# Two pipeline slots earlier: the first expert tiles of a ViT tower beside the last three LSTM steps

## The chip, the cores and the metric

The kernel is one program on one core of one Trainium2 chip. The core has TensorE (PE, matmuls), VectorE (DVE), ScalarE (ACT), GpSimd (POOL) and SyncE (SP, which here only issues DMAs). The metric is the device time of one execution in microseconds (us), the median of three runs of the kernel before.

## The reference, cut to what matters

Three layers on 128 images. Each image becomes T = 65 tokens of width 128 (a class token and 64 patches of 2352 values times W); the tokens are normalized and go through an LSTM over the 65 positions, whose output is added; the sum is normalized again and goes through 16 experts, of which each token uses its best two.

```python
tokens = einsum('bpi,hi->bph', patches, W) + b          # 64 patches an image
h = concat([cls, tokens]) * pos_embed
def step(carry, xt):                                    # 65 steps, one after the other
    gates = xt + h @ W_hh.T
    i, f, g, o = sigmoid, sigmoid, tanh, sigmoid
    c = f * c + i * g;  h = o * tanh(c)
h = h + lstm(layernorm(h))
probs = softmax(xt @ router_w.T + router_b); top 2 of 16
def expert_step(acc, e):                                # 16 experts
    h = gelu(xt @ w1e.T + b1e, approximate=False)       # 128 -> 512
    y = h @ w2e.T + b2e                                 # 512 -> 128
    acc + y * gate
```

## The kernel before, in words

Everything is written as slots n = -5, -4, ..., which each engine goes through in the same order. In a slot an engine runs its part of `step(n)` and, from some slot on, its part of `step_b` for a tile. The function `slots(step, tile)` says how they are put together: up to slot AHEAD = 64 the step comes first and the tile behind it, from slot 65 on the tile first. POOL has its step first in every slot.

`step(n)` is LSTM step n (n = 0 to 64) with all that belongs to it: the projection of the patches of token n+3 (PE L1287, until slot 61), the recurrent matmuls (PE L1297 and L1302), the four gates as tanh (ACT L610), `cab` and `c2` (DVE L809, L812), tanh of the cell (ACT L631), the new hidden state in two float16 parts and one float32 (DVE L831, L833, L837), the transposition of step n-1's hidden state (PE L1312), its sum with the token `h1` (DVE L787), the moments for the norms (DVE L791 to L805), their power -0.5 (POOL L1253), `shift2` (DVE L817), the normalized payload `pay` (ACT L644), the router's logits (PE L1388), and, spread over slots, the router's choice of experts and the ranks of the rows in them (DVE, groups of 8, 6, 4, 4 and 3 tokens). Each token's row is sent twice into the area `sent` of its experts by indirect DMAs on POOL (L1241). What of this belongs to the last tokens stands in slots 65 to 74. A plan, made in pieces on DVE, says for each tile of 256 rows which expert it has and where its rows begin: the early plan (tiles 0 to 23) is read in slot 55, pieces 8 and 9 of it follow in slots 61 and 62, and the late plan (tiles 24 to 79) takes slots 72 to 78, from PLAN_B = 72 on.

`step_b(n)` is tile n of 80. SP loads its rows three slots ahead (`xt`, L537, for which tile j waits for `dst_done` of tile j-4) and the bias b2 one slot ahead (L547, for which tile j waits for `y_done` of tile j-4). One slot ahead PE transposes the rows (L1416) and DVE splits them into two halves (L1113, L1127). In the tile's own slot PE makes the 512-wide layer (L1442, two halves of 6 matmuls of 256 columns), ACT applies gelu (L685, four of 128x256) and rounds to float16 (L694, one of 128x1024), and DVE makes the destination numbers (L1138). One slot later DVE makes the rest (L1105), two slots later PE makes the second layer (L1460, 24 matmuls), three slots later DVE adds the bias (L1120) and POOL scatters the rows into `back` by two indirect DMAs (L1265). Tile 0 is in slot 64: tile n is in slot n + 64.

The first x loads and the matmuls of a tile use memory that the patches had, and PSUM banks that the steps have. So tile 0 waits for the last projection and tiles 0 and 1 for the last gates. SP also writes padding rows behind every expert's rows (L505), two of them in each of eight slots from PLAN_B + 4 on; tile 24's load waits for all of these and for all sent rows.

`warm` (L633) is a gelu of one element at the end of step 64. The instruction that loads ACT's function table for gelu is put before it by the compiler.

Near the end tiles' results are read back in chunks (L511), weighted and added (L674, L1189), and stored (L517).

Of the kernel before, what the change touches and what calls it, by code (L numbers as in the profile page):

```python
# [24 lines left out]
P = 128  # L25
# [28 lines left out]
THIN = 4  # L54
THREE = 3
EARLY = 24
SINGLE_IN, SINGLE_DOWN = 16, 5
AHEAD = 64
assert EARLY <= -(-(2 * P * sum(SIZES[:EARLY_GROUPS]) - E * (ROWS - 1)) // ROWS)
NX = 4  # L60
NPOS = 4
# [36 lines left out]
def tower(nc, x, w, w_rest, cls, pos, w_ih, w_hh, b_ih, b_hh, rw, rb, we, b1, b2, const, out):  # L98
# [3 lines left out]
    with ctx:  # L102
# [147 lines left out]
            return max([i for i in range(j) if alternates(i, single) == alternates(j, single)], default=None)  # L250

        def ps_in(j):
            return bank[6 if alternates(j, SINGLE_IN) else 0][:, 0:ROWS]

        def ps_down(j):
            return bank[4 if alternates(j, SINGLE_DOWN) else 1][:, 0:HALVES * HID]

        def ps_up(n, half):

            return bank[(3, 7, 2, 5)[2 * (n % 2) + half]]  # L260

        def ps_ranks(g, a, b):

# [55 lines left out]
        STARTS = np.cumsum([0] + SIZES).tolist()  # L319
        def slots(step, tile, steps_first=False):  # L320

            for n in range(-5, AHEAD + TILES_B + 4):
                if n <= AHEAD or steps_first:
                    step(n)
                if n >= AHEAD - 3:
                    tile(n - AHEAD)
                if n > AHEAD and not steps_first:
                    step(n)

# [67 lines left out]
        PLAN_AT = {47: 0, 48: 1, 49: 2, 50: 3, 51: 4, 52: 5, 54: 6, 55: 7, 61: 8, 62: 9}  # L397
        LATE_AT = {PLAN_B + k: at for k, at in enumerate(((0,), (1,), (2,), (3,), (4, 5), (6,), (7,)))}
        DIAGONALS_AT = {54: False, PLAN_B + 5: True}
        assert ready(EARLY_GROUPS - 1) < 47 and 52 < ready(EARLY_GROUPS) and 55 <= AHEAD - 3  # L400
        assert PLAN_B + 4 + E // 2 <= AHEAD + EARLY - 3

        def pieces_of(n):

# [41 lines left out]
        def _(sp):  # L446
# [20 lines left out]
            def step(n):  # L467
                t = n + 6
                if 2 <= t <= T - 1:
                    if t <= NX:  # L470
                        sp.wait_ge(ones_in, t)
                    else:
                        sp.wait_ge(tok_done, (t - NX))
                        sp.wait_ge(lo_done, (t - NX))
                    load_patches(t)
                t = n + 4
                if 0 <= t <= T - 1:
                    if t >= NPOS:
                        through(sp, h0_done, t - NPOS)
                    sp.dma_start(posr[:, t % NPOS, :],  # L480
                                 pos[bass.ds(t, 1), :].rearrange("a h -> (a h)").partition_broadcast(P)
                                 ).then_inc(pos_in[t % NPOS], 16)
                if n == -4:
                    for dst, src in ((wih[:, :, :], w_ih), (whh[:, :, :], w_hh),
                                     (lbias[:, 0, :], b_ih), (lbias[:, 1, :], b_hh)):
                        sp.dma_start(dst, src).then_inc(weights_in, 16)
                if n == -3:
                    for dst, src in ((rws[:, :], rw), (rbs[:, :, :], rb.partition_broadcast(P)), (b1s[:, :], b1)):
                        sp.dma_start(dst, src).then_inc(const_in, 16)
                for piece in pieces_of(n + 2):  # L490
                    if piece >= NE:
                        through(sp, ex_lo_done, piece - NE)
                    sp.dma_start(ex_raw[:, piece % NE, :], we[:, bass.ds(piece * PIECE, PIECE)]
                                 ).then_inc(ex_in[piece % NE], 16)
                if n == 10:
                    sp.wait_ge(setup_dve, 2)
                    sp.dma_start(rows_of(sent, E * CAP), pad[:, :, :]).then_inc(pads, 16)
                for e in range(2 * (n - PLAN_B - 4), 2 * (n - PLAN_B - 3)):
                    if not 0 <= e <= E - 1:
                        continue  # L500
                    if e == 0:
                        sp.wait_ge(pad_rows, 1)
                    sp.reg_load(at_pad, padi[0:1, e:e + 1])
                    row = sp.snap(at_pad, min_val=0, max_val=E * CAP - ROWS)
                    sp.dma_start(rows_of(sent, row), pad[:, :, :]).then_inc(pads, 16)  # L505
# [66 lines left out]
        def _(act):  # L572
# [30 lines left out]
            def step(n):  # L603
# [25 lines left out]
                if 0 <= n <= T - 1:  # L629
                    through(act, c_done, n)  # L630
                    act.activation(tc[:, :], c2, ACT.Tanh, scale=0.5).then_inc(tc_done, 1)  # L631
                    if n == T - 1:
                        act.activation(warm[:, :], cst[:, C_ONE:C_ONE + 1], ACT.Gelu)  # L633
                if halved:
                    split(t, KS // 2, KS).then_inc(hi_done, 1)
                if n == -2:
# [22 lines left out]
                for k, (t0, t1, at) in enumerate(SOFTMAX):  # L659
                    if n == at + 1:  # L660
                        exponents(k, t0, t1)

            def exponents(k, t0, t1):

# [24 lines left out]
            def round_off(n):  # L689

                act.wait_ge(gelu_done, 2 * n + 2)
                if n >= 4:
                    through(act, down_ps, n - 4)
                act.activation(hhi[n % 4], pair[n % 2][:, :], ACT.Copy).then_inc(hhi_done, 1)  # L694

            def step_b(n):
                if 0 <= n <= TILES_B - 1:
# [21 lines left out]
        def _(dve):  # L719
# [382 lines left out]
            def remainder(n):  # L1102

                through(dve, hhi_done, n)
                dve.tensor_tensor(hlo[n % 4], pair[n % 2][:, :], hhi[n % 4], ALU.subtract).then_inc(hlo_done, 1)  # L1105

            def step_b(n):
                j = n + 1
# [163 lines left out]
        def _(pe):  # L1272
# [17 lines left out]
            def step(n):  # L1290
# [15 lines left out]
                if 0 <= t <= T - 1:  # L1306
                    through(pe, h_done, t)
                    if t >= 1:
                        through(pe, h1_done, t - 1)
                    if t == T - 1:  # L1310
                        through(pe, yT_done, t - 2)
                    pe.transpose(ps_hT(t), h2[:, t % 2, :], ident).then_inc(h_ps, 1)  # L1312
# [91 lines left out]
            def step_b(n):  # L1404
                j = n + 1
                if 0 <= j <= TILES_B - 1:

                    pe.wait_ge(xt_in[j % 4], (j // 4 + 1) * 16)
                    if j == 0:
                        through(pe, h0_done, T - 1)  # L1410
                    if previous(j, SINGLE_IN) is not None:
                        through(pe, in_done, previous(j, SINGLE_IN))
                    elif j > 0:
                        pe.wait_ge(plan_read, 2)
                    for a in range(HALVES):
                        last = pe.transpose(ps_in(j)[:, a * P:(a + 1) * P], xt[j % 4][:, a, 0:HID], ident)  # L1416
                    last.then_inc(in_ps, 1)
                if 0 <= n <= TILES_B - 1:
# [6 lines left out]
                    through(pe, in_done, n)  # L1425
                    x_hi, x_lo = xTs[n % 2][:, 0:ROWS], xTs[n % 2][:, ROWS:2 * ROWS]
                    for half in range(2):
                        if n >= 2:
                            through(pe, hlo_done, n - 2)
                        elif half == 0:  # L1430
                            through(pe, gates_done, T - 2 + n)
                        elif n == 0:
                            g = max(k for k in range(GROUPS) if ready(k) <= AHEAD)
                            pe.wait_ge(r_dve, g * R + R_MASK + 2)
                            pe.wait_ge(plan_read, 1)
                        else:
                            through(pe, h1_done, T - 2)
# [71 lines left out]
```

## Time and profile before

| | |
|---|---|
| median of 3 runs | 673.73 us (673.32 to 677.51) |
| the profiled execution | 673.6 us, span 671.8 us |
| PE busy | 621.2 us (92%) |
| DVE busy | 562.6 us (84%) |
| ACT busy | 489.5 us (73%) |
| POOL busy | 412.7 us (61%) |

The span is what the profile covers, 1.8 us less than the time of the same execution. Three stretches follow each other: the LSTM steps until 399 us, with the projections beside them until 385.4; the tiles until 651.5; and the last reading back, adding and storing. A busy share is a mean over all three.

### The profile page before, as it was taken

What the parts mean: (1) busy time and instruction counts of PE and PEld (TensorE: products, weight loads), DVE (VectorE), ACT (ScalarE), POOL (GpSimd) and SP (SyncE); (2) the same over time, 40 slices, a digit from 0 to 9 for tenths busy, and PEclk for the clock granted to TensorE, in tenths of its full rate; (3) what the DMA queues carried; (4) which work ended last, traced back from release to release, by engine and by line L of the source; (5) the groups of instructions that cost most, each with busy time, mean ns of one, the idle gap of its engine ahead of it and who ended that gap; (6) DMA issues with size and microseconds to landing.
All of it is one profiled execution on the core that took longest, in us unless ns stands there. A gap on an engine that the chain in (4) does not pass through costs nothing.

```text
span 671.8 us, 24556 instructions
## 1 busy us (share of the span) xinstructions
PE 621.2 (92%) x7952; PEld 588.0 (88%) x7952; DVE 562.6 (84%) x1797; ACT 489.5 (73%) x1259; POOL 412.7 (61%) x446
## 2 busy tenths in 40 slices
PE   5899999999999999999999978999999999999970
PEld 4899999999999999999999957788888989888860
DVE  3877888888888888988989978987777887989896
ACT  3687778666667776665655567777888888999984
POOL 0233333477777776667657777777776666666571
PEclk9999999999999999999999979999999999999995
DMA  8988787677888888877767123456444345555666
GB/s 312 384 293 270 271 276 258 230 259 270 268 276 274 269 270 260 251 232 253 253 217 252 56 64 95 116 155 183 135 119 117 118 109 159 161 171 163 189 223 203
DMA packets 71895, 141.67 MB, mean 211 GB/s; under 512 B 13078, under 2 KB 55650, under 8 KB 63838
## 3 DMA queue, kind: packets, MB, share of 16 engines
q1 hardware_dynamic: 62128, 121.69, 57.0%
q0 software_dynamic: 9280, 17.21, 7.3%
q8 instruction: 70, 1.15, 0.7%
q10 hardware_dynamic: 366, 1.21, 0.5%
q14 instruction: 51, 0.42, 0.2%
HBM read 116.35 MB, written 25.66 MB: 211 GB/s over the span
## 4 chain that ended last, share of the span: by engine, by line
PE 59%; DVE 7%; issue 5%; DMA 5%; SPq 2%; POOL 2%; ACT 1%; POOLq 0%; ACTq 0%; DVEq 0%
PE pair L1287 24%; PE pair L1442 10%; PE pair L1460 10%; PE pair L1333 4%; DMA patches<-sent 4%; PE pair L1297 3%; PE pair L1416 2%; DVE patches L1105 2%; PE pair L1302 1%; POOL back L1265 1%; PE pair L1388 1%; DMA field<-back 1%; PE pair L1322 1%; PE pair L1359 1%; PE pair L1312 1%
## 5 line engine op out<-in xcount | busy, mean ns | idle before, releaser
L1265 POOL DMA_INDIRECT back<-patches x160 | 156.7, 979 | 70.7 <-issue 58.2
L1287 PE MATMUL pair<-field,patches 128*128 128x128 f32 (+1 forms) x1408 | 173.6, 280 | 8.4 <-DMA patches<-in_x 8.4
L1241 POOL DMA_INDIRECT sent<-pay,slot_own x130 | 149.7, 1152 | 40.2 <-issue 38.0
L1287 PEld LDWEIGHTS pair<-field,patches 128*128 128x128 f32 (+1 forms) x1408 | 164.4, 194 | 8.6 <-ACT field L584 6.8
L685 ACT ACTIVATE pair<-pair,b1s 128x256 f32<-128x256 f32 x320 | 123.2, 448 | 31.1 <-PE pair L1442 30.3
L610 ACT ACTIVATE gate<-pair,lbias 128x128 f32<-128x128 f32 x260 | 74.1, 367 | 81.0 <-PE pair L1302 79.1
L1442 PE MATMUL pair<-patches,ex_hi 128*128 128x256 f16 x640 | 111.2, 276 | 6.1 <-DVE patches L1105 3.6
L1460 PE MATMUL pair<-ex_hi,patches 128*128 x1280 | 111.4, 219 | 2.9 <-DVE patches L1105 1.5
L1253 POOL TENSOR_TENSOR rstd<-veps,cst 128x2 f32<-128x2 f32 (+1 forms) x68 | 57.4, 845 | 90.7 <-DVE veps L805 89.5
L1105 DVE TENSOR_TENSOR patches<-pair,patches 128x1024 f16<-128x1024 f32 x80 | 97.0, 1212 | 1.3 <-ACT patches L694 1.3
L1287 PE MATMUL pair<-field 128*128 128x128 f16 x1536 | 96.1, 219 | 0.0
L1460 PEld LDWEIGHTS pair<-ex_hi,patches 128*128 128x128 f16 x1280 | 87.0, 98 | 6.4 <-issue 3.7
L1287 PEld LDWEIGHTS pair<-field 128*128 128x128 f16 x1536 | 91.3, 98 | 0.9
L1460 PE MATMUL pair<-ex_lo,patches 128*128 x640 | 88.0, 219 | 0.0
L1442 PE MATMUL pair<-patches,ex_lo 128*128 128x256 f16 x320 | 87.9, 275 | 0.0
L592 ACT ACTIVATE field<-patches 128x512 f16<-128x512 f32 x128 | 80.7, 632 | 4.5 <-DMA patches<-in_x 4.5
L694 ACT ACTIVATE patches<-pair 128x1024 f16<-128x1024 f32 x80 | 81.9, 1023 | 2.5
L848 DVE TENSOR_TENSOR field<-patches,field 128x1024 f16<-128x1024 f32 x64 | 78.0, 1219 | 0.1
L1442 PEld LDWEIGHTS pair<-patches,ex_hi 128*128 x640 | 55.9, 98 | 24.9 <-issue 14.5
L1215 POOL TENSOR_TENSOR ex_lo<-field,ex_hi 128x256 f16<-128x256 f32 x64 | 45.4, 720 | 43.4 <-ACT field L658 43.0
L1113 DVE CAST patches<-pair 128x256 f16<-128x256 f32 x80 | 33.8, 422 | 35.0 <-PE pair L1416 34.0
L1333 PE MATMUL pair<-xT_hi,wih_hi 128*128 128x128 f16 x260 | 47.4, 220 | 2.9 <-DVE xT_lo L765 2.9
(150 smaller groups left out, 1232.2 us busy)
## 6 DMA issues: line engine op xcount, KB each, us to landing
patches<-in_x SPq DMA_DIRECT2D x62, 1152.0 KB
patches<-sent SPq DMA_DIRECT2D x80, 130.0 KB
field<-in_we SPq DMA_DIRECT2D x64, 128.0 KB
field<-back SPq DMA_DIRECT2D x10, 768.0 KB
patches<-in_b SPq DMA_DIRECT2D x80, 64.0 KB
field<-in_pos SPq DMA_DIRECT2D x65, 64.0 KB
out_tower<-h SPq DMA_DIRECT2D x10, 384.0 KB
back<-patches POOLq DMA_INDIRECT x160
```

The costliest lines, as they stand in the source:

```text
L592: return act.activation(xhi[r][:, a:b, :], xraw[q][:, a:b, :], ACT.Copy)
L610: last = act.activation(gate[:, GATE_AT[g], :], ps_gate[n % 2][:, g * B:(g + 1) * B], ACT.Tanh, bias=lbias[:, 2, g:g + 1], scale=(1.0 if g ...
L685: last = act.activation(up[:, cols], up[:, cols], ACT.Gelu, bias=b1s[:, bass.ds(e * FC + 2 * half + i, 1)], scale=1.0 / E_SCALE)
L694: act.activation(hhi[n % 4], pair[n % 2][:, :], ACT.Copy).then_inc(hhi_done, 1)
L848: dve.tensor_tensor(xlo[r][:, :, :], xraw[q][:, 0:KS, :], xhi[r][:, :, :], ALU.subtract).then_inc(lo_done, 1)
L1105: dve.tensor_tensor(hlo[n % 4], pair[n % 2][:, :], hhi[n % 4], ALU.subtract).then_inc(hlo_done, 1)
L1241: pool.indirect_dma_start(sent, bass.IndirectOffsetOnAxis(ap=slot_own[:, g % 4, choice, col:col + 1], axis=0), pay[:, t % NP, :], None, bo ...
L1265: pool.indirect_dma_start(back, bass.IndirectOffsetOnAxis(ap=dsti[j % NO][:, k:k + 1], axis=0), yo[j % NO][:, k, :], None, bounds_check=2 ...
L1287: last = pe.matmul(bank_of, l, w_, start=(c == KS and k == 0), stop=(c == KS - 1 and k == 2))
L1333: pe.matmul(ps_gate[t % 2][:, g * B:(g + 1) * B], w_[:, g, :], r[:, t % 2, :], start=(g == 0 and k == 0), stop=False, skip_group_check=True)
L1442: last = pe.matmul(ps_up(n, half)[:, i * ROWS:(i + 1) * ROWS], w1, r, start=(k == 0), stop=(k == 2))
L1460: last = pe.matmul(ps_down(j)[:, a * HID:(a + 1) * HID], h, w2, start=(c == 0 and k == 0 and a == 0), stop=(c == FC - 1 and k == 2), skip_ ...
```

## The change

Tile n is in slot n + 62 (`FIRST = AHEAD - 2`), so that tiles 0, 1 and 2 are in slots 62, 63 and 64, behind the LSTM steps of these slots. The steps keep their slots, the padding rows keep their tiles (from slot PLAN_B + 2 on, and so two slots earlier). Because steps 62 to 64 still use their PSUM banks, the first three tiles get others: their rows are transposed into the upper half of the bank of the hidden states, and their 512-wide layer has pair 2, pair 0, pair 1 of banks in turn. The single-element gelu stands at the end of slot 61. Waits follow the banks: the transposition of hidden states 61 to 63 waits for the split of tile 0 to 2, tile 0's layer waits for the last token's `h0`, tile 1's and 2's first half for the gates of steps 63 and 64. From tile 18 instead of 16 on two banks take turns for the transposed rows.

```diff
-SINGLE_IN, SINGLE_DOWN = 16, 5
+SINGLE_IN, SINGLE_DOWN = 18, 5
 AHEAD = 64
+FIRST = AHEAD - 2
+UPPER = 3
...
         def ps_in(j):
+            if j < UPPER:
+                return ps_h[:, 2 * P:2 * P + ROWS]
             return bank[6 if alternates(j, SINGLE_IN) else 0][:, 0:ROWS]
...
+        def ps_pair(n):
+            return pair[(n + 1) % 2 if n else 2]
         def ps_up(n, half):
-            return bank[(3, 7, 2, 5)[2 * (n % 2) + half]]
+            return ps_pair(n)[:, half * 512:(half + 1) * 512]
...
-            for n in range(-5, AHEAD + TILES_B + 4):
+            for n in range(-5, FIRST + TILES_B + 4):
                 if n <= AHEAD or steps_first:
                     step(n)
-                if n >= AHEAD - 3:
-                    tile(n - AHEAD)
+                if n >= FIRST - 3:
+                    tile(n - FIRST)
...
-                for e in range(2 * (n - PLAN_B - 4), 2 * (n - PLAN_B - 3)):
+                for e in range(2 * (n - PLAN_B - 2), 2 * (n - PLAN_B - 1)):
...
-                    if n == T - 1:
-                        act.activation(warm[:, :], cst[:, C_ONE:C_ONE + 1], ACT.Gelu)
...
+                if n == FIRST - 1:
+                    act.activation(warm[:, :], cst[:, C_ONE:C_ONE + 1], ACT.Gelu)
...
-                act.activation(hhi[n % 4], pair[n % 2][:, :], ACT.Copy).then_inc(hhi_done, 1)
+                act.activation(hhi[n % 4], ps_pair(n)[:, :], ACT.Copy).then_inc(hhi_done, 1)
...
-                dve.tensor_tensor(hlo[n % 4], pair[n % 2][:, :], hhi[n % 4], ALU.subtract).then_inc(hlo_done, 1)
+                dve.tensor_tensor(hlo[n % 4], ps_pair(n)[:, :], hhi[n % 4], ALU.subtract).then_inc(hlo_done, 1)
...
                         through(pe, h1_done, t - 1)
+                    if FIRST - 1 <= t < FIRST - 1 + UPPER:
+                        through(pe, in_done, t - FIRST + 1)
...
-                    if j == 0:
-                        through(pe, h0_done, T - 1)
-                    if previous(j, SINGLE_IN) is not None:
+                    if j < UPPER:
+                        through(pe, h1_done, FIRST - 2 + j)
+                    if j == UPPER:
+                        through(pe, hlo_done, 0)
+                    elif previous(j, SINGLE_IN) is not None:
...
-                        if n >= 2:
+                        if n >= UPPER:
                             through(pe, hlo_done, n - 2)
+                        elif n == 0:
+                            through(pe, h0_done, T - 1)
                         elif half == 0:
-                            through(pe, gates_done, T - 2 + n)
-                        elif n == 0:
+                            through(pe, gates_done, T - 3 + n)
+                        elif n == 1:
```

## Rows read from the trace of the kernel before

**Rows 1.** The page's busy times by engine: busy us, share of span, instructions

```profile
PE 621.2 (92%) x7952; PEld 588.0 (88%) x7952; DVE 562.6 (84%) x1797; ACT 489.5 (73%) x1259; POOL 412.7 (61%) x446
```

**Rows 2.** Stretches: length, busy us of PE, PEld, DVE, ACT, POOL, clock, DMA, GB/s

```profile
388.00:390.00 2.00, 0.39 (x5) 0.39 (x6) 1.86 (x9) 0.82 (x3) 1.63 (x2) 1.00 0.31 88
392.00:394.00 2.00, 2.00 (x18) 1.69 (x16) 1.45 (x7) 0.61 (x3) 1.64 (x5) 0.52 0.11 35
...
508.00:540.00 32.00, 32.00 (x416) 28.81 (x413) 26.84 (x59) 27.86 (x55) 20.82 (x23) 1.00 0.40 114
```

**Rows 3.** ACT in order of time: start us, us, line and operation

```profile
386.32 1.14 ACT L610 ACTIVATE gate<-pair,lbias 128x128 f32<-128x128 f32 x4 [1.43 <-PE pair L1302]
...
391.00 1.14 ACT L610 ACTIVATE gate<-pair,lbias 128x128 f32<-128x128 f32 x4 [0.74 <-PE pair L1302]
...
392.96 0.31 ACT L631 ACTIVATE tc<-gate 128x128 f32<-128x128 f32 x1 [0.65 <-DVE gate L812]
394.29 0.49 ACT L644 ACTIVATE pay<-h,shift,rstd 128x128 f32<-128x128 f32 x1 [1.03 <-DVE shift L817]
394.69 1.13 ACT L610 ACTIVATE gate<-pair,lbias 128x128 f32<-128x128 f32 x4
...
397.13 1.28 ACT L633 ACT_TABLE_LOAD   x1
398.43 0.20 ACT L633 ACTIVATE warm<-cst 128x1 f32<-128x1 f32 x1
...
400.88 1.02 ACT L694 ACTIVATE patches<-pair 128x1024 f16<-128x1024 f32 x1
401.80 1.53 ACT L685 ACTIVATE pair<-pair,b1s 128x256 f32<-128x256 f32 x4
...
404.37 1.54 ACT L685 ACTIVATE pair<-pair,b1s 128x256 f32<-128x256 f32 x4
```

**Rows 4.** ACT's groups from 386 to 399 us: busy us, mean ns, idle before

```profile
L610 ACT ACTIVATE gate<-pair,lbias 128x128 f32<-128x128 f32 x12 | 3.4, 367 | 2.2 <-PE pair L1302 2.2
L644 ACT ACTIVATE pay<-h,shift,rstd 128x128 f32<-128x128 f32 x3 | 1.5, 488 | 1.8 <-DVE shift L817 1.8
L631 ACT ACTIVATE tc<-gate 128x128 f32<-128x128 f32 x3 | 0.9, 309 | 2.1 <-DVE gate L812 2.1
```

**Rows 5.** DVE in order of time, from 385 to 441 us

```profile
387.37 0.17 DVE L805 TENSOR_SCALAR veps<-mv 128x2 f32<-128x2 f32 x1
387.50 0.42 DVE L809 SCALAR_TENSOR_TENSOR cab<-gate 128x256 f32<-128x256 f32 x1
...
400.36 0.42 DVE L1113 CAST patches<-pair 128x256 f16<-128x256 f32 x1 [1.17 <-PE pair L1416]
400.82 0.42 DVE L1127 TENSOR_TENSOR patches<-pair,patches 128x256 f16<-128x256 f32 x1
401.93 1.22 DVE L1105 TENSOR_TENSOR patches<-pair,patches 128x1024 f16<-128x1024 f32 x1 [0.69 <-ACT patches L694]
...
433.58 0.41 DVE L1120 SCALAR_TENSOR_TENSOR patches<-pair,patches 128x256 f32<-128x256 f32 x1
...
439.89 0.41 DVE L1120 SCALAR_TENSOR_TENSOR patches<-pair,patches 128x256 f32<-128x256 f32 x1
```

**Rows 6.** The chain of waits in order of time: start us, us, what

```profile
397.23 2.68 PE pair L1442 x12
...
416.21 1.35 PE pair L1442 x12
417.56 1.34 PE pair L1460 x24
```

**Rows 7.** SP in order of time: the first padding rows, the load of tile 24

```profile
441.73 1.19 SPq L505 DMA_DIRECT2D sent<-pad  x2
...
472.37 0.33 SPq L537 DMA_DIRECT2D patches<-sent  x1
```

**Rows 8.** POOL in order of time: the last row sent before tile 24

```profile
447.45 0.97 POOL L1241 DMA_INDIRECT sent<-pay,slot_own  x1 [0.30 <-issue]
```

More of the change, by code:

```diff
@@ L399, in tower @@
         DIAGONALS_AT = {54: False, PLAN_B + 5: True}
-        assert ready(EARLY_GROUPS - 1) < 47 and 52 < ready(EARLY_GROUPS) and 55 <= AHEAD - 3
-        assert PLAN_B + 4 + E // 2 <= AHEAD + EARLY - 3
+        assert ready(EARLY_GROUPS - 1) < 47 and 52 < ready(EARLY_GROUPS) and 55 <= FIRST - 3
+        assert PLAN_B + 2 + E // 2 <= FIRST + EARLY - 3
         def pieces_of(n):
```

## The prediction

> **What bounds the kernel now.** I read the busy times first, and they mislead: PE is busy 92% of the span [rows 1], but the change touches some 20 us around the end of the LSTM, so the question is what ends each wait there. The stretches come next. In 388 to 390 us PE works for 0.39 of 2.00 us, and in 392 to 394 its clock is granted at 0.52, which is the lower of its two levels (1.2 of 2.4 GHz), after that idling [rows 2]. So there is a hole in PE beside steps 62 to 64. Later there is none: from 508 to 540 PE is busy for all 32 us with 416 matmuls; a tile has 38 (2 + 12 + 24), which makes 10.95 tiles and 2.92 us a tile. That is the price of a slot once PE sets the pace.
>
> Then ACT in order of time. The gates of step 63 start at 391.00, those of step 64 at 394.69: a step lasts 3.69 us, and it is a chain of short pieces, gates 1.14, wait 0.65 for `c2`, tanh 0.31, wait 1.03 for `shift2`, pay 0.49, gates again [rows 3]. Step 62 lasts 4.68 (386.32 to 391.00). No engine is full in this chain. ACT's groups show it: from 386.3 it idles for 2.1 + 1.8 us and, of L610's 2.2, for the 0.74 that lie behind 386.32, some 4.7 us in all [rows 3, 4]. From 400.88 on ACT works tile after tile: gelu 401.80, gelu 404.37, a period of 2.57 us [rows 3]. From 401.93 on DVE takes over, as it has the router's work of slots 65 to 78 beside the tiles: its rest of tile 0 starts at 401.93 [rows 5], just behind ACT's rounding (400.88 + 1.02). In slots 76 to 83 SP has the padding rows, two issues of 1.19 us together in each slot beside two loads, the first at 441.73, and tile 24's load goes out at 472.37 [rows 7]. After that PE sets the pace until the tail.
>
> **The change part by part.** The tail and everything from tile 24 on are bound to tile numbers, not slots. So the result is one sum: how much later slot 65 comes (slots 62 to 64 now carry three tiles), against two tile slots less, 2 x 2.92 = 5.84 us.
>
> *The function table.* Load and warm are 1.28 + 0.20 us [rows 3]. They leave the end of step 64, where pay would wait for its shift anyway, and go to the end of slot 61, where ACT idles 1.43 us before 386.32. Cost there 0.05 to 0.2 us, I take 0.1.
>
> *Slot 61, tile 0's rows.* PE's two transposes (some 0.3 us) come before step 62's matmuls, so gates 62 start 0.25 later. DVE's split of the rows takes 400.36 to 401.24, 0.88 us [rows 5], and now stands before DVE's work of step 62. DVE was at its limit there: `veps` 387.37 to 387.54 and `cab` at 387.50 follow each other without a gap [rows 5]. So `c2` and all behind it in step 62 are 0.85 late, and ACT is through with the step at about 391.1.
>
> *Slot 62, tile 0.* PE has its transposes for tile 1 and the reading of the expert's number (0.3 to 0.5 us) and starts the 12 matmuls at about 391.2. They take 2.68 us at the low clock, as tile 0's did at 397.23, and 1.35 at the high one [rows 6]. The first gelu pair needs half of them. With the high clock gelu runs from 391.9, rounding ends at 394.5 (period 2.57), and gates 63 start at 394.6. With the low clock the second half is ready only at 393.9, and gates 63 start at 395.9. Before it was 391.00.
>
> *Slots 63 and 64.* ACT is in program order: gates, tanh, pay, gelu, gelu, rounding, gates. Gelu stands behind pay, and the next gates behind the rounding, so that tile work doesn't go into ACT's waits within a step, it is added: 3.69 + 2.57 = 6.26 us a step. Tile 1's matmuls wait for gates 63 (1.14), then take 1.35 to 2.68: ready at 2.5 to 3.8 after the start of the gates, needed in two halves at 3.69 and 4.5, and so hidden. In the same way tile 2's. Slot 64's rounding ends at 394.6 + 12.5 = 407.1, or 408.4. Before, slot 64's ended at 401.90. DVE has in slot 64 the state (0.9 us after tanh), shift, split 0.88, rest of tile 1 1.22, in slot 65 the split with the bias of tile 0 and reaches the rest of tile 2 at 407.4, which puts the first case up by 0.3. Slot 65 is later by **5.5 to 6.5 us**.
>
> *Slots 65 and 66.* Two things are new there. The bias sum (0.41, of which 0.33 counts as the next overlaps) was not yet there in slot 66's place, and in slot 65 PE has the second layer of tile 1, 1.34 us [rows 6], before the transposition of hidden state 64, for which DVE waits some 0.4. Together 0.7: **6.2 to 7.2 us**. All else that DVE does in slots 65 to 74 is the same as before.
>
> *Padding rows and SP.* SP gets to them in slot 74 instead of 76, released by the bias sum of tile 9. In the old slots 74 and 76 that sum lies at 433.58 and 439.89 [rows 5], 6.31 apart, more than 5.84, since DVE's slots were long. So SP starts 6.2 to 7.2 less 6.31 later, that is 0.1 earlier to 0.9 later, and from there on it has its own work (30.6 us from 441.73 to 472.37 for the same 8 slots [rows 7]) beside which DVE's late plan is hidden; some 0.2 us, in which SP still waited for DVE, can go. That gives **-0.3 to +0.7 us** for tile 24 and for everything behind it. The middle is +0.2.
>
> *POOL.* Its two scatters of a tile come two slots earlier in its queue, so four of them (1.27 us each: 0.97 and 0.30 idle) stand before the last sent rows, 5.1 us. With the 5 us that POOL now waits for the longer steps, the last send goes from 447.45 [rows 8] to 453 to 458. Tile 24 needs it at 472.37: covered by 14 us; if that cover were gone, each further send would cost 1.27. The power that feeds the shift is better off, since steps are longer. The other banks and the change from 16 to 18 cost nothing: the banks that tiles 0 to 2 leave are free when they are needed, and the split of a row tile is done a slot before.
>
> The sum: 673.6 + 0.2 = **673.8 us** for an execution like the profiled one, which is 0.1 below the median of 673.73; I take 673.8.
>
> **The rivals.** *ACT's holes are filled.* If the gates, tanh and gelu of a slot fell so that waits shrink, the bound is ACT's work: 3 tiles x 2.57 = 7.7 us against 4.7 us of idling [rows 4] and the 1.48 of the table that leave this place, 1.5 us more in place of 5.5. Then slot 65 is only 2.2 late, SP starts 6.31 - 2.2 = 4.1 earlier and the time is 669.5. The order gelu behind pay speaks against all of it; half of it would be 671.6. Chance 0.15.
>
> *PE stays slow.* The idling of PE ahead of 390 us brings the low clock [rows 2]. If it stays low through slots 62 to 66, matmuls of a tile end at 4.1 us after its gates start, and those of the next step (0.5 us at the high clock) behind them by another 0.5; three steps and slot 65 make 1.5 to 2 us above my sum: 675.5. It decides once a tile's second half is ready later than 4.5 us after the gates. Chance 0.12.
>
> *The tables.* This is the rival on the slower side. The trace has three table loads; tanh, exp, Copy and Identity ran under the first, gelu, Copy and Identity under the second. No row has a tanh under gelu's table. If it doesn't hold tanh, steps 62 to 64 need a load before their first tanh and one before their gelu: 6 x 1.28 = 7.7 us [rows 3], every one in ACT's chain: 681.2. It decides with the first tanh of step 62. For tanh in the table speaks only that a table held four functions here; chance 0.07. The Trainium skill (ScalarE: Activation LUTs, "Table sets: the hidden batching unit") lists tanh beside exp and beside sigmoid, and for the gelu set no further function, which speaks against this change. By its figure of about 2.66 us a switch (What ACT_TABLE_LOAD costs) the time would be 689.5; the trace has the next instruction 0.02 us behind a load of 1.28.
>
> *The tiles don't move.* If tile 0's chain waits for something that comes with step 64 anyway, slots 62 to 64 stay as they were and the tiles follow as now: 673.6, the same as my forecast to within what can be measured. For tile 4's load this is nearly so: SP waits for tile 0's destination numbers, but needs them later. Chance 0.06.
>
> **How the numbers follow.** My sum has 0.60; its own range is 672.8 to 674.8, the two ends with 0.5 us on both sides for what rows round off. For 8 in 10 the range has to take in half of the first rival and the slow clock: **670.5 to 676.2**; it leaves out the tables and the full filling. A difference below 1% (6.7 us) cannot be told from no change here. Faster by over 1% would need 666.9, below the price of ACT's full filling: 0.02. Slower by over 1% is the table rival: 0.07. Within 1%: 0.91.
>
> **What the new profile would show.** Gates 63 start at 394.6 to 395.9 instead of 391.00, steps 63 and 64 last 6.3 us; the rounding of tile 2 ends at 407 to 408.5; one table load before 386.5 and no other until the last exp; tile 24's load at 472 +- 0.6; PE busy without a gap from there, the same tail. My prediction is wrong if a step with a tile lasts much less than 6.3 us (then ACT's waits were filled), or if SP's padding slots are not the same length as now, which would shift everything behind them.

## The result, and the profile after

The changed kernel takes 677.89 us (median of 20 runs, 673.9 to 679.39) where the kernel before, on the same chips, takes 675.16 (20 runs, 673.32 to 677.51). The ratio is 1.0032, 95% interval 1.0018 to 1.0045: some 2.2 us slower, clear of zero and far inside 1%. The median of the three runs shown ahead of the prediction lay low (673.73). The profiled execution has a span of 675.4 us, 3.6 more than before.

All times below are read against the tanh of the cell in step 61, the last piece on ScalarE ahead of the moved work. It starts at 382.28 us before and at 382.93 here. This 0.65 is no effect of the change: over the executions profiled below the same piece starts 0.03 to 1.67 late, also where nothing ahead of slot 76 differs. I take it off and call what is left "later" or "earlier".

ACT in order of time in the changed kernel, against [rows 3]:

```profile
382.93 0.31 ACT L639 ACTIVATE tc<-gate 128x128 f32<-128x128 f32 x1 [1.14 <-DVE gate L820]
...
385.56 1.28 ACT L669 ACT_TABLE_LOAD   x1
...
393.17 0.81 ACT L693 ACTIVATE pair<-pair,b1s 128x256 f32<-128x256 f32 x2 [1.42 <-PE pair L1456]
394.24 0.81 ACT L693 ACTIVATE pair<-pair,b1s 128x256 f32<-128x256 f32 x2 [0.26 <-PE pair L1456]
395.08 1.02 ACT L702 ACTIVATE patches<-pair 128x1024 f16<-128x1024 f32 x1
396.00 1.14 ACT L618 ACTIVATE gate<-pair,lbias 128x128 f32<-128x128 f32 x4
...
402.29 1.14 ACT L618 ACTIVATE gate<-pair,lbias 128x128 f32<-128x128 f32 x4
403.29 0.30 ACT L627 ACTIVATE ynT<-pair 128x128 f32<-128x128 f32 x1
...
407.25 0.81 ACT L693 ACTIVATE pair<-pair,b1s 128x256 f32<-128x256 f32 x2 [0.25 <-PE pair L1456]
408.09 1.02 ACT L702 ACTIVATE patches<-pair 128x1024 f16<-128x1024 f32 x1
```

Gates 63 come at 396.00, that is 4.35 later than the 391.00 of before; gates 64 at 402.29, 6.95 later; step 63 lasts 6.29 us instead of 3.69. Gates 63 follow the rounding of tile 0 without a wait. One table load, and no other in steps 62 to 64.

The chain of waits from gates 64 on, against [rows 6]:

```profile
402.29 1.14 ACT gate L618 x4
403.42 0.18 ACT ynT L627
403.60 0.04 issue
403.64 0.61 PE pair L1398 x2
404.25 0.51 PE pair L1428 x2
404.76 2.35 PE pair L1456 x12
407.11 1.34 PE pair L1474 x24
408.45 0.23 PE pair L1428 x2
```

Here is what the sum of the prediction left out. After gates 64 the chain leaves ScalarE for TensorE: the logits wait for `ynT`, which stands behind the gates, and then TensorE has one queue of the rows of tile 3, tile 2's first layer at the low clock (2.35 us), tile 0's second layer and the rows of tile 4. The stretches show the clock, against [rows 2]:

```profile
400.00:402.00 2.00, 0.62 (x8) 0.39 (x5) 1.94 (x6) 1.97 (x5) 1.44 (x2) 1.00 0.10 33
402.00:404.00 2.00, 0.36 (x2) 0.36 (x3) 0.85 (x4) 1.59 (x6) 1.34 (x2) 0.83 0.44 107
404.00:406.00 2.00, 2.00 (x11) 1.39 (x11) 1.49 (x7) 0.70 (x2) 1.39 (x3) 0.50 0.20 66
406.00:408.00 2.00, 2.00 (x26) 1.74 (x24) 1.63 (x3) 1.67 (x5) 1.70 (x2) 0.81 0.21 69
```

PE works 0.98 of the 4 us from 400 to 404 (from 400.6 to 403.6 it does nothing), and its clock is granted at 0.50 in the next two, the lower level. VectorE gets the rows of tile 4 late, against [rows 5]:

```profile
408.71 0.42 DVE L1121 CAST patches<-pair 128x256 f16<-128x256 f32 x1 [1.09 <-PE pair L1428]
...
409.72 1.21 DVE L1113 TENSOR_TENSOR patches<-pair,patches 128x1024 f16<-128x1024 f32 x1
```

The rest of tile 2 (slot 65) starts at 409.72, 7.14 later than slot 65's rest of before (401.93). Before, it followed ScalarE's rounding at once; here the rounding ends at 409.11, and VectorE comes 0.6 after it, because it waited for the rows of tile 4 from TensorE. The slot after it is 7.8 later, and every slot up to 78 then 7.8 to 8.1 later. Two slots at the pace of the padding stage are not enough to give this back, as SP shows, against [rows 7]:

```profile
444.04 1.20 SPq L513 DMA_DIRECT2D sent<-pad  x2
...
450.95 2.16 SPq L513 DMA_DIRECT2D sent<-pad  x2
...
475.34 0.33 SPq L545 DMA_DIRECT2D patches<-sent  x1
```

The first padding rows are 1.66 later than before, tile 24's load 2.32 later. From there the two kernels run in step: VectorE's rest of tile 24 is 2.44 later, that of tile 60 2.29, that of tile 79 2.89.

### The profile page after: what moved, and what is told of

The parts are those of the page before. It is cut to its first block, busy times and chain, and to the rows that moved or that the text cites. A ratio compares the mean times of both kernels' runs of the same rounds, so it can differ in the third digit from the quotient of the medians.

```text
span 675.4 us, 24556 instructions
## 1 busy us (share of the span) xinstructions
PE 622.1 (92%) x7952; PEld 589.6 (87%) x7952; DVE 562.5 (83%) x1797; ACT 490.2 (73%) x1259; POOL 412.7 (61%) x446
## 4 chain that ended last, share of the span: by engine, by line
PE 59%; DVE 7%; DMA 6%; issue 6%; POOL 2%; ACT 1%; SPq 1%; POOLq 0%; ACTq 0%; DVEq 0%
PE pair L1295 24%; PE pair L1456 10%; PE pair L1474 10%; DMA patches<-sent 4%; PE pair L1343 4%; PE pair L1305 3%; PE pair L1428 2%; DVE patches L1113 2%; PE pair L1310 1%; POOL back L1273 1%; PE pair L1398 1%; DMA field<-back 1%; PE pair L1332 1%; PE pair L1369 1%; PE pair L1322 1%
## 5 line engine op out<-in xcount | busy, mean ns | idle before, releaser
L1474 PEld LDWEIGHTS pair<-ex_lo,patches 128*128 128x128 f16 x640 | 49.2, 98 | 0.0
```

Source lines behind the costliest of these rows:

```text
L1474: last = pe.matmul(ps_down(j)[:, a * HID:(a + 1) * HID], h, w2, start=(c == 0 and k == 0 and a == 0), stop=(c == FC - 1 and k == 2), skip_ ...
```

## The experiments

The twelve runs are compared in a few places: VectorE's rest of tile 2, of tile 14 (in the padding stage), of tile 24 (behind it) and of tile 79, each in us later (+) or earlier (-) than the same tile in the kernel before. The stage from the first padding rows to tile 24's load, in us, says what SP's slots cost. The ratio is over 11 or 12 timed runs each (20 for the changed kernel), against the kernel before on the same chip.

| kernel | tile 2 | tile 14 | tile 24 | tile 79 | stage | ratio (95%) |
|---|---|---|---|---|---|---|
| before | 0 | 0 | 0 | 0 | 30.6 | 1 |
| changed | -1.22 | +1.13 | +2.44 | +2.89 | 31.3 | 1.0032 (1.0018 to 1.0045) |
| 1 table only | -0.25 | -0.16 | +0.16 | +0.37 | 30.8 | 0.9996 (0.9977 to 1.0014) |
| 2 one slot | +0.95 | +1.92 | +4.11 | +4.91 | 32.4 | 1.0041 (1.002 to 1.0063) |
| 3 ScalarE lags | -2.06 | +0.45 | +2.33 | +4.85 | 31.3 | 1.0023 (1.0001 to 1.0045) |
| 4 second layer early | -1.37 | +1.95 | +4.26 | +5.33 | 32.1 | 1.004 (1.002 to 1.0059) |
| 5 before, padding split | -0.19 | -0.08 | -1.57 | -0.38 | 28.9 | 0.9968 (0.995 to 0.9986) |
| 6 changed, padding split | +0.41 | +2.52 | +0.91 | +1.81 | 29.0 | 1.0005 (0.9986 to 1.0024) |
| 7 recurrence first | -2.84 | -0.27 | +0.36 | +0.67 | 30.5 | 1.0004 (0.9986 to 1.0023) |
| 8 = 7, padding split | -3.52 | -0.95 | -2.39 | -1.78 | 28.3 | 0.9981 (0.9963 to 1.0) |
| 9 changed, again | +0.25 | +2.63 | +3.58 | +7.99 | 30.8 | 1.0053 (1.0035 to 1.0072) |
| 10 clock kept up | -2.54 | +0.08 | +3.19 | +4.50 | 31.7 | 1.0038 (1.002 to 1.0055) |
| 11 = 8, clock kept up | -3.64 | -1.11 | -2.83 | -0.20 | 27.7 | 0.9978 (0.9962 to 0.9995) |
| 12 = 11, padding earlier | -3.69 | -1.13 | -2.89 | -1.53 | 30.4 | 0.9973 (0.9958 to 0.9988) |

In the kernel before, VectorE's rest of tile 2 comes 8.36 us behind that of tile 0, so 0 in the column "tile 2" would be a slot 65 that is 8.36 us later, and -1.22 is the 7.14 above. The stage of number 12 is one slot longer than the others, as its padding rows start a slot earlier for the same tile 24.

Each row is one execution, and one program differs from execution to execution. The changed kernel was profiled twice (+2.44 and +3.58 at tile 24), and up to tile 11 number 6 is a third execution of it: tile 2 lies at -1.22, +0.25 and +0.41. Behind tile 63, while results are read back, it is worse: number 9 loses 4.5 us between tiles 63 and 74 and number 3 2.8. So the readings go by tiles 2 to 24, differences of about 1 us between two rows settle nothing by themselves, and the ratio says what is left of them.

**1. The table load alone.** The kernel before, and only the load moved:

```diff
-                    if n == T - 1:
-                        act.activation(warm[:, :], cst[:, C_ONE:C_ONE + 1], ACT.Gelu)
...
+                if n == AHEAD - 3:
+                    act.activation(warm[:, :], cst[:, C_ONE:C_ONE + 1], ACT.Gelu)
```

> The kernel before with one part of the change: the single-element gelu, and so the load of its table, stands at the end of slot 61, and the tiles stay in slots 64 and on. If gelu's table holds tanh (my theory), there is one load before 386.5 us and none in steps 62 to 64, gates 62 start at most 0.2 us late, the rounding of tile 0 ends 0 to 0.4 us earlier than 401.9, and the time is that of before within 0.5 us. If it doesn't, three pairs of loads of 1.28 us stand in steps 62 to 64 and the time is 4 to 8 us longer.

The load is at 385.62 us, the twelve gates and three tanh behind it run with no other load, and the tiles are 0.25 earlier up to tile 13. The table that is loaded for gelu serves tanh too. The rival of the tables is out, and this part costs nothing that can be measured (0.9996).

**2. One slot instead of two.** `FIRST = AHEAD - 1`, tiles 0 and 1 with the banks of before, tile 0's rows in the bank of the hidden states, padding rows from PLAN_B + 3 on:

```diff
-FIRST = AHEAD - 2
-UPPER = 3
+FIRST = AHEAD - 1
+UPPER = 1
...
-            return pair[(n + 1) % 2 if n else 2]
+            return pair[n % 2]
```

> The change with one slot instead of two: tile n in slot n + 63, tiles 0 and 1 beside steps 63 and 64. Theory 'added, not hidden': a step with a tile lasts 6.3 us instead of 3.7, so slot 65 comes 3.3 to 4.0 us later than before for one tile slot of 2.92 won, and tile 24 is loaded 0.3 to 1.2 us later than before, half of the 2.3 us of the full change. Rival 'padding rows': what is lost is lost in SP's slots, whose number is the same; then the loss of tile 24 is near the full 2.3 us. Rival 'one hole is free': the first tile fits into waits, and tile 24 comes earlier than before.

Slot 65's rest is 3.51 later, inside the 3.3 to 4.0, but the one behind it is 4.77 later, and for tile 24 no side's number came: it is 4.11 later, more than in the full change. The first padding rows are 2.00 later; 1.8 us more arose in the padding stage (32.4 us instead of 30.6). The profile shows no clock fall in step 63 here, but one after step 64: TensorE does nothing from 397.0 to 400.3, and the clock is granted at 0.50 from 400 to 406 us. One tile beside the steps was enough for such a wait, and the time is no better than that of the full change (1.0041 against 1.0032, the intervals overlap).

**3. ScalarE lags.** In the changed kernel ScalarE's part of tiles 0 and 1 goes into the waits of steps 63 and 64, the first half of gelu ahead of the cell's tanh, the second behind it, the rounding behind `pay`; VectorE's rest of tile 0 now stands in step 64, ahead of its wait for the gates:

```diff
+                lagging = n - FIRST - 1 if FIRST < n <= T - 1 else None
+                if lagging is not None:
+                    e = expert_at(lagging)
+                    gelu(lagging, 0, e)
                 if 0 <= n <= T - 1:
...
                     act.activation(tc[:, :], c2, ACT.Tanh, scale=0.5).then_inc(tc_done, 1)
+                if lagging is not None:
+                    gelu(lagging, 1, e)
...
+                if lagging is not None:
+                    round_off(lagging)
```

> The change, with ScalarE's part of tiles 0 and 1 put one slot later and into its waits: in steps 63 and 64 the first gelu pair stands before tanh of the cell, the second behind it, the rounding behind pay; tile 2 follows in slot 65 before tile 3, and VectorE's rest of tile 0 stands before the first product of step 64. If ScalarE's program order is what makes a step with a tile 6.3 us long, gates 63 start at about 392.5, steps 63 and 64 last 4.6 to 5.2 us, and the rest of tile 2 on VectorE starts at 404.5 to 406 instead of 409.7; tile 24 is loaded 3 to 4.5 us earlier than in the change, and the time is 0.5 to 2.5 us below before. If the slots behind 64 or SP's padding rows are the bound, the gain is gone by tile 24 and the time is that of the change, 2 to 3 us above before.

Half of what was expected came. Step 63 lasts 4.61 us (396.15 to 400.76), as expected. But gates 63 don't come sooner:

```profile
396.15 1.15 ACT L618 ACTIVATE gate<-pair,lbias 128x128 f32<-128x128 f32 x4 [4.28 <-PE pair L1325]
...
400.76 1.13 ACT L618 ACTIVATE gate<-pair,lbias 128x128 f32<-128x128 f32 x4
```

ScalarE waits 4.28 us for the recurrent matmuls of step 63 (L1325 here), which stand behind tile 0's first layer on TensorE (12 matmuls in 2.5 us, at the low clock). So gates 63 come at the same time by either of two orders, ScalarE's and TensorE's. Taking away one leaves the other. My expectation had only one.

**4. Second layer of tile 0 in step 64's hole**, in TensorE's step ahead of the logits:

```diff
+                if n == FIRST + 2:
+                    second_layer(0)
```

> The change, with one piece moved: the second layer of tile 0 (24 matmuls) stands in step 64 on TensorE, ahead of the logits, in the 3.0 us in which TensorE waited, instead of behind tile 2's first layer. If the low clock and this order cost what I read from the profile, TensorE keeps its high clock, tile 2's 12 matmuls take 1.35 instead of 2.35 us, and the rest of tile 2 starts 0.9 to 1.5 us earlier (408.2 to 408.8 by the profile of the change); tile 24 and the end gain as much. If ScalarE alone sets the pace there, the gain is at most 0.3 us.

Counted as above, tile 2's rest is only 0.15 earlier than in the changed kernel, which looks like a miss. But this execution came late to the edit: up to step 64 the program is the changed kernel, and tile 0's first layer happened to take 2.7 us instead of 1.9, so that gates 63 and 64 start 0.84 and 0.89 later than in the first profile. From gates 64 on it did what was expected:

```profile
402.80 1.13 ACT gate L618 x4
...
409.20 1.23 DVE L1113 TENSOR_TENSOR patches<-pair,patches 128x1024 f16<-128x1024 f32 x1
```

The clock stays at the high level from 396 to 414 us, tile 2's first layer takes 1.48 us, and the rest of tile 2 comes 6.4 us after gates 64 and at once behind ScalarE's rounding. In the three executions with the order of the change it comes 7.4, 8.0 and 9.0 us after gates 64. Further on the gain is lost (+4.26 at tile 24): TensorE slows at 414.8 us (24 matmuls of the second layer in 2.04 us), and the padding stage takes 32.1 us. The time is not better (1.004).

**5 and 6. Every second padding DMA on ScalarE's queue** (the lines with `e` odd stand in ScalarE's step), in the kernel before and, with `PLAN_B - 2` for `PLAN_B - 4`, in the changed one:

```diff
-                for e in range(2 * (n - PLAN_B - 4), 2 * (n - PLAN_B - 3)):
+                for e in range(2 * (n - PLAN_B - 4), 2 * (n - PLAN_B - 3), 2):
...
+                e = 2 * (n - PLAN_B - 4) + 1
+                if 0 <= e <= E - 1:
...
+                    act.reg_load(at_pad, padi[0:1, e:e + 1])
+                    row = act.snap(at_pad, min_val=0, max_val=E * CAP - ROWS)
+                    act.dma_start(rows_of(sent, row), pad[:, :, :]).then_inc(pads, 16)
```

> The kernel before; every second padding-row DMA is issued by ScalarE's queue instead of SyncE's, in the same slots. If SyncE's issuing (3.5 to 4.2 us a slot, eight slots) is what sets the pace from tile 12 to tile 24, a slot there falls to VectorE's or TensorE's 2.95 to 3.5 us, tile 24 is loaded 2 to 4 us earlier than 472.4, and the time falls by as much. If what is slow is the DMA engines' own work on the padding rows (16 DMAs of 130 KB), it is the same within 0.7 us.

> The changed kernel with the same edit. Theory 'two losses': 1.5 us come from slots 62 to 65 and are there before the padding rows, 0.8 us come in SyncE's slots. With SyncE relieved, tile 24 is 2.5 to 4.5 us earlier than in the change, and against the kernel before with the same edit the loss is what VectorE's slots give, 0.5 to 1.9 us. Rival 'it is all SyncE': the two kernels with this edit are equal within 0.5 us at tile 24.

Tile 24 comes 1.57 earlier in the kernel before and 1.53 earlier in the changed one (+0.91 instead of +2.44). SP's issuing does set the pace there, for less than I expected (2 to 4 and 2.5 to 4.5). And the change costs as much with the padding split as without: 2.48 and 2.44 us at tile 24, by the ratios 0.37% and 0.32% (so close an agreement at tile 24 is luck, as one program differs by more). So the rival "it is all SyncE" falls, and so does my theory's 0.5 to 1.9; what is lost with the padding split is made ahead of the padding rows (first rows 2.98 later, stage 29.0 against 28.9) and passed on. Number 5 is faster than the kernel before, clear of zero. Number 6 also shows chance: it is the changed kernel until slot 74, yet its tile 2 is 1.6 later than in the first profile, and its low clock lasted longer. The chain has tile 2's first layer in 2.56 us and tile 0's second layer in 2.56 as well:

```profile
404.22 2.56 PE pair L1464 x12
406.78 2.56 PE pair L1482 x24
```

**7 and 8. The recurrence first**, on both engines, without and with the split padding. Tile n - 63's first layer stands on TensorE behind step n's recurrent matmuls, the first half of its gelu on ScalarE behind the cell's tanh, and the rest behind `pay`; VectorE's rest of tile 0 as in number 3:

```diff
+                if n in (FIRST + 1, FIRST + 2):
+                    first_layer(n - FIRST - 1)
...
                     act.activation(tc[:, :], c2, ACT.Tanh, scale=0.5).then_inc(tc_done, 1)
+                if lagging is not None:
+                    e = expert_at(lagging)
+                    gelu(lagging, 0, e)
...
+                if lagging is not None:
+                    gelu(lagging, 1, e)
+                    round_off(lagging)
```

> The change with both orders turned round in steps 63 and 64: TensorE does the recurrent matmuls of the step first and the first layer of the tile before (tile 0 in step 63, tile 1 in step 64) behind them; ScalarE does its gelu behind tanh of the cell, one slot later than in the change, tile 2 following in slot 65. If gates 63 started late (396.0) only because TensorE did tile 0's 12 matmuls at the low clock first, they start at 391.8 to 392.8 now, and gates 64 at 397.5 to 399 instead of 402.3. The rest of tile 2 starts 1.5 to 4 us earlier than in the change, and tile 24 1 to 3.5 us earlier. If what is taken out there only comes back behind slot 64, tile 24 is the same within 0.7 us.

> The kernel of the third run with the padding rows split between SyncE and ScalarE as in the first two. If the two losses are independent, it gains over the change what the two edits gain alone, 4 to 7 us at tile 24, and is 1.5 to 4 us faster than the kernel before. If one hides the other, it is no better than the better of the two.

ACT in number 7:

```profile
392.35 1.14 ACT L618 ACTIVATE gate<-pair,lbias 128x128 f32<-128x128 f32 x4 [0.79 <-PE pair L1324]
...
396.57 0.81 ACT L700 ACTIVATE pair<-pair,b1s 128x256 f32<-128x256 f32 x2 [0.77 <-PE pair L1479]
...
399.44 1.14 ACT L618 ACTIVATE gate<-pair,lbias 128x128 f32<-128x128 f32 x4
```

Gates 63 start 0.9 later than before instead of 4.35, gates 64 4.3 later instead of 6.95. Tile 2's rest is 1.6 earlier than in the changed kernel, tile 24's 2.1: the loss of the change is gone (+0.36, ratio 1.0004), and so it came from the order in the queues in steps 62 to 64. Step 63 did not get shorter by this (7.09 us, as tile 0's matmuls still met the low clock, 0.50 from 394 to 396); what was won is that it starts 3.5 us sooner. TensorE's order was not turned round alone: number 3 has ScalarE's and VectorE's, number 7 all three. With the padding split too, tile 24 is 2.39 earlier than before, 4.83 earlier than in the changed kernel, more than the two edits gained alone (2.1 and 1.5). The time, 0.9981, is 1.3 us better than before, a little less than the 1.5 to 4 I expected, and its interval reaches to no difference.

**9 and 10. The changed kernel again, and with the clock kept up** by matmuls of no use:

```diff
+                if n == 64:
+                    through(pe, r_logits, 8)
+                for _ in range({62: 34, 64: 38}.get(n, 0)):
+                    pe.matmul(ps_logit[:, 256:384], wih_hi[:, 0, :], wih_hi[:, 1, :], start=True, stop=True,
+                              skip_group_check=True)
```

> The changed kernel as it is, once more, beside the next two. It says how far one execution differs from another: I expect gates 63 at 4.2 to 4.5 us later than before, counted from step 61's tanh, slot 65's rest 6.9 to 8.5 us later, as TensorE's low clock in slots 64 and 65 ends at another moment in each execution, and tile 24 2 to 4 us later.

> The changed kernel with matmuls that do nothing of use (float16, 128 columns, into columns nobody reads) on TensorE in its two waits: 34 in step 62 behind the ranks, 38 in step 64 ahead of the logits. If the low clock costs what I read, the clock stays at the high level, tile 0's and tile 2's 12 matmuls take 1.35 to 1.5 us instead of 1.9 and 2.35, gates 63 start 0.4 to 1.2 us earlier, and slot 65's rest on VectorE 1.3 to 2.5 us earlier than in the change; tile 24 gains as much and the loss against before falls from 2.4 to 0 to 1.1 us. If the clock is only a companion of waits that ScalarE's order sets, slot 65 is the same within 0.4 us.

Number 9 was expected at 4.2 to 4.5 for gates 63 and has 5.11; its slot 65, at 8.61, lies just above 8.5. The stretches of number 10 have the clock at 1.00 from 388 to 412 us. Gates 63 start at 395.16, which is 4.03 later than before (4.35 in the first profile, 5.11 in number 9), step 63 lasts 6.28 as ever, and tile 2's rest is 1.32 earlier than in the first profile and 2.79 earlier than in number 9. Against number 6 it is 2.95. So the low clock costs 1.3 to 2.95 us in slots 62 to 65 of the changed kernel, and differs by 1.6 from one execution to the next. As in number 4, the rest of tile 2 follows ScalarE's rounding at once in number 10; in the first profile, number 9 and number 6 it comes 0.6, 1.4 and 2.0 after it. In number 9 the low clock sits later:

```profile
404.00:406.00 2.00, 1.42 (x10) 1.08 (x11) 1.37 (x5) 0.56 (x3) 1.70 (x2) 0.94 0.38 119
406.00:408.00 2.00, 2.00 (x15) 1.59 (x13) 1.97 (x5) 1.63 (x4) 1.39 (x3) 0.50 0.16 50
408.00:410.00 2.00, 2.00 (x25) 1.96 (x24) 0.28 (x3) 1.50 (x3) 1.61 (x2) 0.71 0.26 58
```

The gain is still there at tile 14 (+0.08) and then it goes: tile 24 is 3.19 later. That part of the expectation failed. The chain of number 10 says where:

```profile
459.85 4.14 DMA patches<-sent
...
467.99 2.66 DMA patches<-sent
...
471.64 4.03 DMA patches<-sent
```

Two loads of rows land 4.0 and 4.1 us after their issue, one lands after 2.66, and one issue held SP for 1.60 us instead of 0.35. But the chain of number 7 has a load of 4.42 and that of number 5 one of 5.25, and they lose little or nothing there, so slow loads alone don't explain it. The time isn't measurably better than that of number 9 on the same chip (1.0038 and 1.0053, the intervals overlap): that the clock costs time is shown up to tile 14, not at the end.

**11 and 12.** Number 8 with 34 such matmuls in step 62, and then the padding rows from slot 73 instead of 74:

```diff
-                for e in range(2 * (n - PLAN_B - 2), 2 * (n - PLAN_B - 1), 2):
+                for e in range(2 * (n - PLAN_B - 1), 2 * (n - PLAN_B), 2):
```

> The version with the recurrence first and the padding rows split, with 34 such matmuls in step 62. If they keep the clock up through steps 62 and 63, tile 0's first layer takes 1.35 instead of 2.7 us, step 63 gets 0.5 to 1.5 us shorter, and tile 24 comes 3 to 4 us earlier than before instead of 2.4. If tile 0 is not what step 63 waits for, it is the same as without them within 0.4 us.

> The version with the recurrence first, the clock kept up and the padding rows split, with the padding rows one slot earlier (from slot 73, right behind the slot in which their places are known). In the version before tile 24's load went out 3.9 us behind tile 23's, as it waited for the last padding rows to land. If that wait is on the path, tile 24 comes another 1 to 2.5 us earlier (5 to 6 us earlier than in the kernel before at its load, 3.8 to 5.3 at its rest) and the time is 0.3 to 0.6% below before. If the DMA engines are what is short there, the wait only moves and tile 24 is the same within 0.5 us.

Number 11: the clock is up, tile 2's rest is 0.12 earlier than in number 8, tile 24's 0.44. Tile 0 was hardly what step 63 waited for once the recurrence stood first. Step 63 did not get shorter (6.58 us, 6.04 in number 8). Number 12, SP:

```profile
465.30 0.33 SPq L545 DMA_DIRECT2D patches<-sent  x1
...
468.48 0.33 SPq L545 DMA_DIRECT2D patches<-sent  x1
```

The first is tile 23's, the second tile 24's. It goes out 3.2 us behind tile 23's instead of 3.9, 4.46 earlier than before and 1.0 earlier than in number 11, and the rest of tile 24 doesn't move (0.06). In both profiles the chain from 455 us on is TensorE's matmuls, tile after tile, past tile 24: that wait was not on the path. The ratio is 0.9973, the best of the versions with moved tiles, 1.8 us below the kernel before; number 5, which moves no tile, has 0.9968. The intervals of numbers 5, 8, 11 and 12 overlap, so which is best isn't settled. In the profiles of numbers 11 and 12 some of the lead is lost again (from -2.8 and -2.9 at tile 24 to -1.0 and -1.2 at tile 60), more than half of it behind tile 50; why is not shown.

## Why the prediction was right and wrong

**The median of before.** The range was set around 673.73, three runs; twenty gave 675.16. The measured 677.89 lies 1.7 above the upper end of 676.2. The ratio, which is free of this, gives +2.2 us where +0.1 to +0.2 was forecast. Put on 673.73 that is 675.9, inside the range, which had been made wide for the slow clock, but above the 674.8 of the sum's own range. So the low median put the time outside the range, and a missing 2 us in the sum is what the rest of this part is about.

**The function table.** Right: one load, no measurable cost, and tanh under gelu's table in the changed kernel and in number 1. The list in the Trainium skill (ScalarE: Activation LUTs, "Table sets: the hidden batching unit"), which names no tanh for the gelu set, is no complete list: here the measurement decides. The load took 1.28 us, as before.

**Slots 61 and 62.** Nearly right in size: gates 63 were said to start at 394.6 to 395.9. Counted as above they start at 395.35, 395.44, 396.11 and 396.19 in four executions (the changed kernel, numbers 6, 9 and 4) and at 395.03 with the clock kept up. So the lower end was 0.4 too early, and with tile 0 wholly at the low clock the upper end was 0.2 to 0.3 too early. Not foreseen: TensorE's order alone would have made them as late (number 3, tile 0 at the low clock).

**Slots 63 and 64: the step that failed.** "A step of 6.26 us" was right (6.29), and so was the end of tile 2's rounding: 407.1 to 408.4 was said, 408.46 measured, counted as above. What failed is "ready at 2.5 to 3.8 after the start of the gates [...] and so hidden. In the same way tile 2's." For tile 1 it held: its gelu waits for nothing. Tile 2's 12 matmuls end 4.8 after the start of gates 64 (402.29 to 407.11). In step 64 TensorE had idled for 3.0 us, since the logits wait for `ynT` behind gates behind the rounding, so its clock fell; and I counted for slot 65 what ScalarE and VectorE have to do, not that VectorE waits for the rows of tile 4, which stand on TensorE behind tile 2's first layer and tile 0's second. Slot 65 was said to be 5.5 to 6.5 later and is 7.14, and 8.6 and 8.8 in numbers 9 and 6. Number 10, with the clock up, has 5.82, inside what I said: the order on TensorE is harmless at the high clock. So this term is short by the low clock, which costs 1.3 to 2.95 us there; beyond the upper end of 6.5 it is 0.6 to 2.3. It is the rival "PE stays slow", with its price about right (1.5 to 2 us) and its chance of 0.12 too small: its own sign, a second half ready later than 4.5 us after the gates, came in step 64, the idling of before [rows 2] spoke for it, and the change made a wait of 3.0 us.

**Slots 65 and 66.** 0.7 was said, 0.66 measured.

**Padding rows and SP.** The link was right: SP started 1.66 later, which is 7.8 to 8.1 less 6.31. Wrong was that 0.2 us could go there, the second term that failed: the stage took 31.3 us, not 30.4. The later start of the padding rows (1.66 instead of 0.4) and these 0.9 us are the 2.1 us by which tile 24's load missed the forecast (2.32 later instead of 0.2). Over the seven executions with moved tiles and all padding on SP it took 30.5 to 32.4, 31.5 on average, against 30.6 and 30.8 with tiles in their old slots. What can be seen are pairs of padding issues that take up to 2.6 us instead of 1.2. POOL's last sends reach further into this stage: to 460.18 in the changed kernel, counted as above, instead of 447.45. They are not the whole cause, if they are one: in number 7 the last send is at 458.80 and the stage takes 30.5, and in number 1, where it stays at 447.2, two padding issues are long too (0.83 and 0.76 us instead of 0.35). No run takes the sends out, and the cause of these 0.9 us stays open.

**POOL.** The last send was said to go to 453 to 458 and went to 460; it still had 14 us to tile 24, and no wait for it shows.

**The tail.** "The same tail": +2.44 at tile 24 and +2.89 at tile 79 in the profiled execution.

## What to carry to other kernels

Work put beside a chain of short dependent steps is hidden only if it stands in each engine's queue behind what the chain needs next. At the end of a step on ScalarE and TensorE it was added whole (6.29 us a step instead of 3.69); reordering the queues of TensorE, ScalarE and VectorE took the loss back (tile 24 from +2.44 to +0.36), reordering ScalarE and VectorE alone left it (+2.33). When a wait on TensorE gets longer, price the matmuls behind it at the low clock too. And before work is moved ahead of a stage that another queue paces, relieve that stage: splitting 16 padding DMAs over two queues gave 0.9968, while the moved tiles gave at best 1.0004 without that split and 0.9973 with it.

## What the runs showed of the hardware that was not expected

The granted clock fell to 0.50 behind 3.0 us in which TensorE did nothing (400.6 to 403.6 in the changed kernel), and how long it then stayed there differed between executions of the same program: 12 plus 24 matmuls took 2.35 and 1.34 us in one and 2.56 and 2.56 in another. In number 10, 34 and 38 small matmuls in the waits held it at 1.00 throughout.

A DMA issue on SP, mostly 0.35 us in the padding stage, took up to 1.76 us (numbers 2 and 4), and pairs of 1.2 us took up to 2.6, while padding rows, row loads and POOL's scatters ran together.
